# Attention sums of both query halves in one PSUM bank, seven rotating banks, and moved transfers in a fused image-and-text block

## The reference

```python
p = patches(x)                                  # 784 patches of 8x8x3 for each image
h = p @ W_embed + b_embed + positions
for i in range(3):                              # graph layers on the 28x28 grid
    hw = h @ W_gcn[i]
    h = relu(normalised_neighbour_sum(hw) + b_gcn[i])
h = concat([h @ W_out + b_out, txt], axis=1)    # 861 tokens of 64
n = layernorm(h)
q, k, v = heads(n @ Wq.T + bq), ...             # 4 heads of 16
h = h + bf16(softmax(q k^T / 4) v) @ Wo.T + bo  # 861 x 861 attention per head
n = layernorm(h)
h = h + shared_mlp(n) + sum over the top 2 of 4 experts of weight * expert_mlp(n)
```

## Time and profile before

| quantity | value |
|---|---|
| median of three runs | 5438.16 us |
| time of the profiled execution | 5431.24 us |
| its span, first to last instruction | 5429.4 us |
| mean granted TensorE clock | 0.932 |
| PE busy | 4924.5 us (91%) |
| VectorE busy | 3488.8 us (64%) |
| ScalarE busy | 3009.4 us (55%) |
| GpSimd busy | 1264.1 us (23%) |
| DMA | 386.00 MB, mean 71 GB/s |

### The profile page before, as it was taken

How to read it: one execution, slowest core, us unless ns; L and a number is a source line. 1 busy time by engine, 2 the same in 40 slices (tenths; PEclk the granted TensorE clock), 3 DMA queues, 4 the chain that set the end, 5 groups by cost and what they waited for, 6 DMA issues and landing times.

```text
span 5429.4 us, 81305 instructions
## 1 busy us (share of the span) xinstructions
PE 4924.5 (91%) x29710; PEld 3279.8 (60%) x29710; DVE 3488.8 (64%) x7660; ACT 3009.4 (55%) x6161; POOL 1264.1 (23%) x1169
## 2 busy tenths in 40 slices
PE   5388999999999999999999999999999999999997
PEld 3255665666665666666566666566666656666654
DVE  3166666666666666666766666766666676666674
ACT  0035556556655655555555565565655555556565
POOL 1112222122222212222222222221222222222112
PEclk8689999999999999999999999999999999999998
DMA  1332332332333233233232233333323333323220
GB/s 42 86 78 62 88 74 72 80 72 70 75 86 72 74 80 68 69 81 78 71 76 66 70 80 81 73 78 77 71 69 82 79 73 73 80 66 71 53 44 6
DMA packets 193397, 386.00 MB, mean 71 GB/s; under 512 B 74986, under 2 KB 118634, under 8 KB 193002
## 3 DMA queue, kind: packets, MB, share of 16 engines
q1 hardware_dynamic: 191978, 379.91, 30.9%
q10 hardware_dynamic: 1024, 0.89, 0.1%
HBM read 309.13 MB, written 109.26 MB: 77 GB/s over the span
## 4 chain that ended last, share of the span: by engine, by line
PE 55%; issue 14%; DMA 11%; DVE 7%; SPq 6%; ACT 3%; POOL 2%; POOLq 0%; DVEq 0%; ACTq 0%; another core or an unknown queue 0%
PE ps L1129 10%; PE ps L1141 9%; PE ps L1120 9%; DMA k_stack<-qk_scratch 8%; PE ps L1177 7%; SPq L637 6%; DVE neg_max_halves L893 5%; PE ps L1195 4%; PE ps L1259 3%; PE ps L1168 3%; PE ps L1153 2%; PE ps L1238 2%; PE ps L1183 2%; DMA image_rows<-image_by_row 2%; ACT probs L777 1%
## 5 line engine op out<-in xcount | busy, mean ns | idle before, releaser
L893 DVE TENSOR_REDUCE neg_max_halves<-ps 123x1 f32<-123x432 f32 (+1 forms) x3584 | 2026.2, 598 | 928.4 <-PE ps L1141 912.0
L777 ACT ACTIVATE probs<-ps 123x432 f32<-123x432 f32 x3584 | 1700.0, 540 | 898.4 <-PE ps L1120 865.9
L1141 PE MATMUL ps<-k_stack,q_stack 96*123 96x432 f32 x3584 | 1353.2, 413 | 236.3 <-DMA k_stack<-qk_scratch 212.2
L1120 PE MATMUL ps<-q_stack,k_stack 97*123 97x432 f32 x3584 | 1277.7, 402 | 48.1 <-ACT probs L777 17.7
L1141 PEld LDWEIGHTS ps<-k_stack,q_stack 96*123 96x123 f32 x3584 | 671.6, 195 | 625.3 <-issue 469.4
L1120 PEld LDWEIGHTS ps<-q_stack,k_stack 97*123 97x123 f32 x3584 | 666.6, 193 | 338.9 <-issue 120.7
L1129 PE MATMUL ps<-probs,v_and_one 123*32 123x432 f32 x7168 | 815.4, 570 | 15.0 <-ACT probs L777 15.0
L840 ACT ACTIVATE hidden<-ps,plain_w 128x432 f32<-128x432 f32 x640 | 397.2, 629 | 216.0 <-PE ps L1195 215.3
L1177 PE MATMUL ps<-adjacency,parts_hi 112*128 112x392 f32 x1344 | 463.2, 345 | 3.2 <-DVE parts_lo L915 3.2
L1177 PE MATMUL ps<-adjacency,parts_lo 112*128 112x392 f32 x1344 | 459.6, 342 | 0.0
L1129 PEld LDWEIGHTS ps<-probs,v_and_one 123*32 123x32 f32 x7168 | 188.9, 114 | 404.3 <-issue 283.1
(11 more groups left out here) (156 smaller groups left out, 6331.1 us busy)
## 6 DMA issues: line engine op xcount, KB each, us to landing
image_rows<-image_by_row SPq DMA_DIRECT2D x256, 586.9 KB
q_stack<-qk_scratch SPq DMA_DIRECT2D x256, 216.0 KB, 7.8
k_stack<-qk_scratch SPq DMA_DIRECT2D x256, 216.0 KB, 8.1
image_by_row<-in_x SPq DMA_DIRECT2D x192, 196.0 KB
qk_scratch<-parts_hi SPq DMA_DIRECT2D x64, 432.0 KB, 2.5
qk_scratch<-parts_lo SPq DMA_DIRECT2D x64, 432.0 KB, 3.3
out<-tokens SPq DMA_DIRECT2D x64, 215.2 KB
tokens_next<-in_txt SPq DMA_DIRECT2D x64, 19.2 KB
```

The costliest lines, as they stand in the source:

```text
L777: act.activation(P[:, (g * 2 * NB + unit) % SLOTS, h, :], T[0:BLK, 0:HW], ACT.Exp, scale=SCALE).then_inc(free[r], 1)
L893: v.tensor_reduce(NM[:, qb * HEADS + h, half:half + 1], T[0:BLK, 0:keys], AX.X, ALU.max, negate=True).then_inc(free[r], 1)
L1120: mm = pe.matmul(T[0:BLK, 0:cn], KS[:, g % 2, h, kb * BLK:(kb + 1) * BLK], QS[:, g % 2, h, c0:c0 + cn], start=True, stop=True)
L1141: mm = pe.matmul(T[0:BLK, 0:cn], QS[0:SHIFT_ROW, g % 2, h, qb * BLK:(qb + 1) * BLK], KS[0:SHIFT_ROW, g % 2, h, c0:c0 + cn], start=True, st ...
```

## The change

The sums of both halves go to bank 4, one after the other, and bank 5 joins the rotation. `pv` is issued at other places: units 0-1, 2-3 and 4-5 at n = 2, 4, 6 as before, unit 6 (the last of the first half) alone at n = 8, then units 7-8, 9-10, 11-12 at n = 9, 11, 13 and unit 13 alone at the end. The eviction of the first half stands in the list ahead of unit 7. The store of an image becomes a step of its own, later than `back`. Most tables change; `FETCH` is 0.725 image earlier.

```diff
 def attention_steps(g):
     units = [(half, kb) for half in range(2) for kb in range(NB)]
-    out, due = [], []
+    groups, out, due = {2: (0, 2), 4: (2, 4), 6: (4, 6), 8: (6, 7), 9: (7, 9), 11: (9, 11), 13: (11, 13)}, [], []
     for n, unit in enumerate(units):
         for h in range(HEADS):
             out.append(("s", g, *unit, h))
             if h == 1:
                 out += due
                 due = []
-                if n and n % 2 == 0:
-                    out.append([("pv", g, *one) for one in units[n - 2:n]])
-                    due = [("oev", g, half) for half, kb in units[n - 2:n] if kb == NB - 1]
-    return out + [[("pv", g, *one) for one in units[2 * NB - 2:]], ("wait", 0.1), ("oev", g, 1)]
+                if n in groups:
+                    done = units[groups[n][0]:groups[n][1]]
+                    out.append([("pv", g, *one) for one in done])
+                    due = [("oev", g, half) for half, kb in done if kb == NB - 1]
+    return out + [("pv", g, *units[-1]), ("wait", 0.1), ("oev", g, 1)]
...
-MAX = ((-0.693, 0.158), (-0.638, 0.167))
-FINISH = ((1.016, 1.084), (1.072, 1.165))
+MAX = ((-0.693, 0.158), (-0.598, 0.167))
+FINISH = ((1.016, 1.084), (1.072, 1.148))
 NORM_M = ((1.109, 1.222), (1.167, 1.195))
-EXPERT = ((1.374, 1.997), (1.266, 1.872))
-GATE = ((1.464, 1.665), (1.347, 1.401))
-BIAS = ((1.602, 1.743), (1.581, 1.692))
-NORM_A = ((-1.483, -1.351), (-1.672, -1.474))
-PROJECT = ((-1.307, -1.271), (-1.361, -1.284))
-STACK = ((-1.043, -0.983), (-1.082, -0.936))
-VALUE = (-1.013, -0.998)
+EXPERT = ((1.374, 1.987), (1.267, 1.882))
+GATE = ((1.464, 1.648), (1.347, 1.356))
+BIAS = ((1.602, 1.743), (1.585, 1.71))
+NORM_A = ((-1.492, -1.426), (-1.672, -1.474))
+PROJECT = ((-1.335, -1.274), (-1.361, -1.246))
+STACK = ((-1.03, -0.99), (-0.995, -0.93))
+VALUE = (-1.017, -1.003)

 GRAPH = (-2.077, -1.521)
-PACK = (-4.046, -3.564, -3.331, -2.611)
-FETCH = -4.95
-LOAD_LEAD, EMBED_LAG = 0.144, 0.22
+PACK = (-4.041, -3.658, -3.428, -2.792)
+STORE = (2.545, 2.592)
+FETCH = -5.675
+LOAD_LEAD, EMBED_LAG = 0.132, 0.224
...
-            + [(g + VALUE[b], ("v", g))])
+            + [(g + VALUE[b], ("v", g)), (g + STORE[b], ("store", g))])
...
-            bank = (0, 1, 2, 3, 6, 7)[turn % 6]
+            bank = (0, 1, 2, 3, 5, 6, 7)[turn % 7]
             turn += 1
         elif st[0] == "pv" and st[3] == 0:
-            bank = 4 + st[2]
+            bank = 4
...
-                    elif kind == "back":
-                        emptied(sp, turn, st)
+                    elif kind == "store":
+                        emptied(sp, turn, ("back", st[1]))
```

More of the change, by code:

```diff
@@ L295, in build @@
         ps = ctx.enter_context(nc.psum_tensor("ps", [128, 8, 512], F32))
-        acc = ps[:, 4:6, :]
+        acc = ps[:, 4, :]
         W = sb("plain_w", [128, PLAIN_W - EMB_W], F32)
@@ L651, in run @@
                 for b in range(2):
-                    stored = sum(st[0] == "back" and st[1] % 2 == b for st in steps)
+                    stored = sum(st[0] == "store" and st[1] % 2 == b for st in steps)
                     if stored:
@@ L813, in run @@
                         filled(act, turn, ("pv", g, half, 0))
-                        act.activation(OT[:, half * HW:(half + 1) * HW], acc[:, half, 0:HW], ACT.Copy
-                                       ).then_inc(free[4 + half], 1)
+                        act.activation(OT[:, half * HW:(half + 1) * HW], acc[:, 0:HW], ACT.Copy
+                                       ).then_inc(free[4], 1)
                     elif kind == "obt":
@@ L882, in run @@
                 hb_no = ranks(steps, lambda st: st[0] == "hb" and st[2] == 2 * EXPERTS)
-                out_no = [ranks(steps, lambda st: st[0] == "back" and st[1] % 2 == b) for b in range(2)]
+                out_no = [ranks(steps, lambda st, b=b: st[0] == "store" and st[1] % 2 == b) for b in range(2)]
                 for st in steps:
@@ L1000, in run @@
                         v.wait_ge(full[r], n)
-                        counted(v, out_dma[g % 2], out_no[g % 2], ("back", g - 2), 16)
+                        counted(v, out_dma[g % 2], out_no[g % 2], ("store", g - 2), 16)
                         v.tensor_tensor(H[:, :, g % 2, :], T[0:BLK, 0:NB * HID].rearrange("p (k f) -> p k f", f=HID),
@@ L1128, in run @@
                         for h in range(HEADS):
-                            pm = pe.matmul(acc[32 * h:32 * h + 32, half, 0:HW], VV[:, g % 2, kb, h, :],
+                            pm = pe.matmul(acc[32 * h:32 * h + 32, 0:HW], VV[:, g % 2, kb, h, :],
                                            P[:, slot, h, :], start=kb == 0, stop=kb == NB - 1,
@@ L1132, in run @@
                         if kb == NB - 1:
-                            pm.then_inc(full[4 + half], 1)
+                            pm.then_inc(full[4], 1)
                         else:
```

## The result

The changed kernel takes 5216.25 us (median of four runs, 5210.61 to 5217.86), the kernel before 5435.17 us beside it: ratio 0.9595, 95% interval 0.9579 to 0.9612, some 219 us or 4.1% less. The profiled execution has a span of 5208.7 us against 5429.4, and a mean granted clock of 0.941 against 0.932. The forecast was 5130 in a range of 5000 to 5330.

A forecast was written before the change was run, and what follows sets the result against it. PE, 91% busy, was taken as the bound, losing time to stack-load waits and a halved clock. Terms -305 - 80 - 40 + 111 + 30 - 25 = -309 from 5431.2 gave 5122, with 6.9 added 5129, rounded to 5130 us; range 5000 to 5330.

The forecast's parts named there:

- moved transfers: Loads, fetch and store around the even image's stack load: PE's wait for it ends; -330 us with the start.
- stack stop: PE's `mx` waits for the even image's stack load, 31 of 5.65 us after the start, vanish: -175 us.
- lost clock behind it: PE's slow work at half clock after each wait for the stack load goes: 31 x 4.2 = -130 us.
- second fall: Clock drop at `wb` beside the even layernorm "a", claimed mostly ended by moving that layernorm: -80 us.
- seventh bank: PE's score weight loads wait less for banks, as each step may lag one more eviction: -40 us.
- one bank: new wait, groups: Sums of both halves share a bank: wait before unit 7 +90, regrouped `pv` +13, end +8; +111 us.
- computing tables: Shorter odd gate and even layernorm chains on VectorE hold up `mx` evictions, `hb` may be late: +30 us.
- rival C: ScalarE and VectorE caught up during the stack stop; half its gain returns as bank waits: about 5400 us, chance 0.09.
- bunching: Dependent VectorE steps crowd together, delaying `mx` evictions, and `hb` may be late: +30 us, bounds 0 to +80.
- added wait: Unit 7's `pv` waits for `oev` of the first half, 1.4 us in each of 64 images: +90 us.
- Rival A: The new wait before unit 7 drops the clock; slower, 5647 us with a fall in all 64 images; chance 0.08.
- Rival B: The stack still lands last, leaving stops of one or two us that drop the clock: 5311 us, chance 0.14.

## Why the prediction was right in sum, and where it was wrong

| step | forecast | measured |
|---|---|---|
| moved transfers with the start, whole | -330 | -219 in the span, transfers alone |
| of it the stack stop, idle | -175 | -174 |
| of it the lost clock behind it | -130 | -145 with the transfers alone, some 28 of them inside the stops |
| of it the start | -25 | its wait went from 37.2 to 25.0 us; not separated |
| second fall | -80 | PE's stops at `wb` gone, clock not; +0.6% when moved alone |
| seventh bank | -40 | some -110 on the new tables; with its groups a cost on the old |
| one bank: new wait, groups | +111 | -70 when the wait is taken away |
| computing tables | +30 | +2.7% with six banks, -1.8% with the new banks and the earlier `oev` (second fall included) |
| all but the moved transfers | +21 | -2 in the span |
| whole | -309 | -219 |

**The moved transfers** are the term that was mis-sized, and the miss is there: -330 forecast with the start, -219 measured with the transfers alone. The mechanism was right, and so were the two main parts: the stops are gone, and the full-speed work lost went from 369 to (1 - 0.957) x 5210 = 224 us. But the two can't be added up to a gain in time: 190 us of stops (with the start) and 145 us of lost clock went, and the span became only 219 us shorter. Of the 116 us between, some 28 (31 x 0.9) are low clock inside the stops, where it cost nothing. Another 54 are in PE's stops behind VectorE, which sum to 160 us in that kernel instead of 106; the row of `wb` above is the largest part of them. The rest stays open. This is what rival C said: the stop was also time in which VectorE caught up. C had half of the gain lost again; less than a third was (219 against 305).

**Within this term** moving the load alone removed 126 of the 212 us, the fetch nothing, and the store alone made it worse. I had read the 6.51 us issue as what the load did. The store-only run shows that the issue is blocked only where a store stands behind the load, and that ending the block alone gained nothing.

**The rest of the change** came out near the forecast in sum (+21 against -2) by luck. The second fall did not end: the layernorm moved alone left the clock as it was and cost 0.6%. The seventh bank and the computing tables were both far off in size. They are one thing, since each costs alone and together they gain: with the tables for computing VectorE falls behind, and the bank bridges that. My bound of +80 for bunching was too low for six banks.

**The clock** over the whole change was off by some 125 us: -130 and some 57 of the -80 were forecast, -62 came. The stack's falls went as forecast, but the rest of the change brought 307 - 224 = 83 us of falls back, one of 3.4 us in nearly every image. That they come from evictions crowding around the transposes, `l2` and `wb` is argued and not shown.

**The added wait** was sized well: 90 forecast, and 70 in time when it was taken away, together with 39 us less of full-speed work lost. It can be avoided by moving `oev`. Rival A was wrong for the new tables, where most falls stay without the wait, and right for the old ones, where the bank part alone made the kernel slower. **Rival B** did not come true, in the pair shown by 0.1 us; two waits of 1.2 us together are left of it.

## What to carry to other kernels

When an engine stops once in a period for a transfer, look in the issuing queue first for what is ahead of the transfer, and for what is ahead of the transfers that it depends on. Here 4% came from moving transfers alone, moving the one behind gained nothing, and one of the moves made alone cost 2%. Don't add a stop and the lost clock behind it up to a gain: 190 us of stops and 145 us of lost clock went here, and the span became 219 us shorter, in part because another engine had used the stop to catch up. And when one evicted bank is to serve two groups in turn, put its eviction into the evicting engine's order ahead of the work that depends on the latest matmuls.

## What the runs showed of the hardware

- The image-row load moves 99 GB/s on a DMA share of 0.27, and a stack queued 10 us behind it lands 23.7 to 28.1 us after its release; with the queue empty it is 17.5 us. The Trainium skill ("DMA: Bandwidth & Descriptors", Why a DMA increments its semaphore by 16 and not by 1) says that a transfer is spread over the largest number of engines up to 16 that divides the slowest dimension of both its sides; here these are 4 shifts and 96 partitions, so 4 engines of 16, and the share of about a quarter agrees.
- SyncE's first stack issue behind an output store was long wherever a row load was still ahead of both (6.51, 6.59 and 1.93 us), and ended 16.8 to 18.8 us after that load's issue each time. It took 0.34 us with the load ahead and no store, and 0.33 us with neither.
- The same VectorE cast took 1.56 us beside GpSimd's packing, and 0.43 us in the median of its 128 executions in the same kernel; in the mean it went from 817 to 581 ns when moved away from the packing.
